# A decoder kernel with another order of norms and distance pieces in its time-warping stage, and a quantised feed-forward written as one pipeline over 16 token tiles

## The chip, the core and the metric

The kernel runs on one core of a Trainium2 chip. The metric is the device time of one launch in microseconds, the median over several runs. Five engines matter: PE (TensorE, matrix products and transposes, results in PSUM), DVE (VectorE), ACT (ScalarE), POOL (GpSimd) and SP (SyncE, which here only issues DMAs). They run independently and wait for each other through semaphores.

## The reference, cut to what matters

Two layers are computed on x (4 batches, 512 tokens, 256 features) with a context of 4 x 1024 tokens. The change touches the first and the last of four sublayers.

```python
# layer 0, cross part: dynamic time warping of layernorm(x) (512) against the context (1024)
D = sqrt(maximum(aa + bb - 2.0 * (a @ b.T), 0))      # aa, bb: squared norms of the rows
row[j] = D[i, j] + minimum(minimum(up, left), diag)  # 512 rows, a scan along 1024 columns
# backtrack the cheapest path, add the rows of one along it to the other, gated

# layer 1, feed-forward: everything is rounded to 4-bit floats in blocks of 16
scale = maximum(max(abs(xb)) / 6, 1e-12)             # per block of 16 features
q(x)  = sign(x) * grid(abs(x / scale)) * scale
h = silu(q(layernorm(x)) @ q(w_gate).T) * (q(layernorm(x)) @ q(w_up).T)   # 704 wide
x = x + tanh(g) * (q(h) @ q(w_down).T)
```

Between them lie a causal self-attention with a mixture of experts and a masked cross-attention, which the change leaves alone.

## The kernel before

The program is a row of blocks (`nc.Block()`). In a block each engine has its own hand-written list of instructions; the next block starts when all engines have finished theirs.

**The time-warping front.** After the inputs have been transposed, `dtw_block` runs `layer_norm` (DVE) on x, turns the result with `transpose_tokens` into `xnT` (scaled by -2), and then runs `dtw_norms`, a block of its own: DVE squares pieces of 512 columns, PE sums them over partitions with a stationary operand of two columns, DVE adds a constant row. The norms of the context go out to memory and come back as one number per partition and lane (`norms`); those of x stay as `rows_j`.

**The distances and the scan** share one block, `dtw_costs`. The 512 rows of x are "slots". They are worked on in cuts of `WIDE` = 112 slots (112, 112, 112, 112, 64). A cut has RB = 33 distance tiles. A tile is 8 PE products of 32 stationary columns each, placed side by side in the array (four batches x two halves of the features), and 4 more that add `rows_j`; four PSUM buffers hold tiles. For the first cut DVE adds the norm and clips (L357), ACT takes the root (L460). For later cuts ACT does both (`rectify` L449, `root` L456). Then ACT's queue stores the cut to memory (`store`, L439), and SP loads it back in chunks of CH = 16 slots in another layout (L316), since the scan runs skewed over 32 lanes per batch.

The scan is DVE's: a turn works off one chunk, 36 turns in all, each 16 times a minimum, a lane shuffle and a scan, with the path rules of the chunk before mixed in. After each turn ACT copies the chunk's decisions away (`keep`, L430 and L432). DVE may not write the decisions of the next turn but one before that is done (`kept`). ACT's list is written out: 11 rectifies ahead of each keep in three turns, the four roots and the store in the fourth.

**The feed-forward.** `fp4_ffn` loads the weights, normalises x, and rounds eight pieces in one block with `quantize` (`ffq_`): four of weights and four of x (1024 wide each). `Quantizer` is spread over three engines for each piece: DVE finds the maxima, scales and inverts them (`scale`, L1873 to L1876); POOL multiplies x by the inverse and the sign by the maximum (`divide`, L1901 and L1905); ACT gives sign and absolute value; DVE rounds by three instructions (`grade`, L1882 to L1884); POOL multiplies the two halves (`combine`, L1911). `lead` says how many pieces `scale` runs ahead of `grade`, and the buffers are lead + 1. Then `turn_rows` transposes the weights and `transpose_tokens` the rounded x.

After that a loop of four passes (`nc.Fori(0, B)`) takes a batch each, as four token tiles of 128: PE makes gate and up products in two halves of 352 columns (L2064), ACT silu (L2106), DVE multiplies (L2130), the quantiser with lead 1 and two buffers rounds the 704 hidden features (`ffb_`), PE transposes them (L2077), ACT copies (L2117 to L2122), PE multiplies with the down weights (L2087), DVE adds to x (L2140).

Of the kernel before, what the change touches and what calls it, by code (L numbers as in the profile page):

```python
# [158 lines left out]
def dtw_block(nc, d, x_sb, ident, ctxT, ctxT_d):  # L159
# [3 lines left out]
    norms_d = nc.dram_tensor("ctx_norms", [1, B * PADI], F32).ap()  # L163
    with ExitStack() as es:
        near = es.enter_context(nc.sbuf_tensor("near", [P, RB, TROW], F16))
        above = es.enter_context(nc.sbuf_tensor("above", [P, RB, TROW], F16))
        with ExitStack() as es1:
            xnT = es1.enter_context(nc.sbuf_tensor("xnT", [P, DH, B * S], F32))
            with ExitStack() as es2:
# [4 lines left out]
            rows_j = es1.enter_context(nc.sbuf_tensor("rows_j", [2, B, S], F32))  # L174
            norms = es1.enter_context(nc.sbuf_tensor("norms", [P, RB], F32))
            dtw_norms(nc, d, xnT, ctxT, rows_j, norms, norms_d)
            dtw_costs(nc, d, dist, near, above, xnT, ctxT, ctxT_d, rows_j, norms, x_sb)
# [3 lines left out]
def dtw_norms(nc, d, xnT, ctxT, rows_j, norms, norms_d):  # L181

    with ExitStack() as es:
        sq = es.enter_context(nc.sbuf_tensor("sq", [P, 2, 2, 512], F32))
        ones2 = es.enter_context(nc.sbuf_tensor("ones2", [P, 2, 2], F32))
        add2 = es.enter_context(nc.sbuf_tensor("add2", [2, 2], F32))
        rows_i = es.enter_context(nc.sbuf_tensor("rows_i", [2, B, PADI], F32))
        ps_n = [es.enter_context(nc.psum_tensor(f"ps_n{i}", [P, 512], F32)) for i in range(2)]
        consts = es.enter_context(nc.semaphore("d_consts"))
        squared = es.enter_context(nc.semaphore("squared"))  # L190
        normed = es.enter_context(nc.semaphore("normed"))
        norm_kept = es.enter_context(nc.semaphore("norm_kept"))
        filled = es.enter_context(nc.semaphore("d_filled"))
        stored = es.enter_context(nc.semaphore("d_norms_stored"))
        spread = es.enter_context(nc.semaphore("d_norms_spread"))

        jobs = [(0, b, c, 1.0) for b in range(B) for c in range(0, SK, 512)] + [(1, b, 0, 0.25) for b in range(B)]
        with nc.Block() as block:
            def keep_norm(dve, n):
                w, b, c, f = jobs[n]  # L200
                if n == 0:
                    dve.wait_ge(consts, 32)
                    dve.wait_ge(filled, 2)
                dve.wait_ge(normed, n + 1)
                dst = rows_j[:, b, :] if w else rows_i[:, b, LEAD + c:LEAD + c + 512]
                nc.vector.tensor_scalar(dst, ps_n[n % 2][0:2, :], add2[:, w:w + 1], None,
                                        ALU.add).then_inc(norm_kept, 1)

            @block.sync
            def _(sp):  # L210
                sp.dma_start(ones2[:], d["c_ones2"]).then_inc(consts, 16)
                sp.dma_start(add2[:], d["c_add2"]).then_inc(consts, 16)
                sp.wait_ge(norm_kept, 2 * B)
                sp.wait_ge(filled, 2)
                sp.dma_start(norms_d, rows_i[0:1, :, :].rearrange("o b i -> o (b i)")).then_inc(stored, 16)
                sp.wait_ge(stored, 16)
                sp.dma_start(norms[:, :], norms_d.rearrange("o (p r) -> (o p) r", r=RB)).then_inc(spread, 16)
                sp.wait_ge(spread, 16)

            @block.gpsimd  # L220
            def _(pool):

                nc.gpsimd.memset(rows_i[:, :, :], 1.0).then_inc(filled, 1)
                pool.wait_ge(filled, 1)
                nc.gpsimd.memset(rows_i[0:1, :, 0:LEAD], FAR2).then_inc(filled, 1)

            @block.vector
            def _(dve):
                for n, (w, b, c, f) in enumerate(jobs):
                    if n >= 2:  # L230
                        dve.wait_ge(normed, n - 1)
                    for h in range(DH):
                        src = xnT[:, h, b * S:(b + 1) * S] if w else ctxT[:, b, h, LEAD + c:LEAD + c + 512]
                        i = nc.vector.scalar_tensor_tensor(sq[:, n % 2, h, :], src, f, src, ALU.mult, ALU.mult)
                    i.then_inc(squared, 1)
                    if n >= 1:
                        keep_norm(dve, n - 1)
                keep_norm(dve, len(jobs) - 1)

            @block.tensor  # L240
            def _(pe):
                pe.wait_ge(consts, 32)
                for n, (w, b, c, f) in enumerate(jobs):
                    pe.wait_ge(squared, n + 1)
                    if n >= 2:
                        pe.wait_ge(norm_kept, n - 1)
# [2042 lines left out]
```

## Time and profile before

| | |
|---|---|
| median of 3 runs | 2692.8 us (2691.69 to 2695.81) |
| the profiled execution | 2694.47 us |
| its span (first to last instruction) | 2692.7 us |
| mean granted TensorE clock | 0.784 of full speed |
| busy share of the span | PE 66%, DVE 61%, ACT 36%, POOL 10% |

The profiled execution took 1.8 us more than its span. The shares are averages over stages that are bound by different engines, so what a change in one stage is worth has to be read from that stage's own stretch of the trace. PE's clock has two levels, 1.2 GHz (0.5 in the profile) and 2.4 GHz (1.0).

### The profile page before, as it was taken

The page shows a single profiled execution, that of the slowest core. Times are in us where ns is not written, and L with a number is a line of the kernel's source. Part 1 is how long each engine was busy: PE and PEld are TensorE (multiplying, and loading weights), DVE is VectorE, ACT ScalarE, POOL GpSimd, SP SyncE. Part 2 cuts the span into 40 slices and gives each one's busy share as a digit, 9 for nine tenths or more (in the row PEclk, how much of TensorE's full clock was granted, in tenths as well). Part 3 has the DMA queues.
Part 4 walks back from the last instruction along what each step waited for, and adds up shares of the span by engine and source line. Part 5 has one row for each costly group of instructions (what it writes and reads, how often), then busy time and mean ns, then how long its engine had stood idle before and what let it go on. Part 6 is the DMA issues. An engine that isn't in the chain of part 4 may idle for free. (4 is left out here: it accounts for less than half of the span.)

```text
span 2692.7 us, 39964 instructions
## 1 busy us (share of the span) xinstructions
PE 1789.7 (66%) x13193; PEld 1032.5 (38%) x13272; DVE 1647.0 (61%) x6787; ACT 982.2 (36%) x1794; POOL 260.3 (10%) x224
## 2 busy tenths in 40 slices
PE   5989500170837888832979507999999999604675
PEld 2445300010724555421656405444544543303453
DVE  5397899898658888440101146767667676286544
ACT  1244522220015666500212002666666666313322
POOL 0000000000000000013000220000000000064432
PEclk8555555555958999955989857999999999857888
DMA  3211100300010000025041122100100000100000
GB/s 96 110 61 51 70 28 28 109 0 1 16 45 9 9 9 2 1 81 192 24 146 49 49 78 86 55 2 1 56 1 25 1 1 1 33 0 0 0 0 31
DMA packets 60244, 104.90 MB, mean 39 GB/s; under 512 B 7449, under 2 KB 42703, under 8 KB 58407
## 3 DMA queue, kind: packets, MB, share of 16 engines
q1 hardware_dynamic: 42654, 72.91, 7.9%
q10 hardware_dynamic: 14352, 22.28, 2.3%
q0 software_dynamic: 3072, 7.53, 0.9%
q8 instruction: 100, 1.64, 0.3%
q14 instruction: 66, 0.54, 0.1%
HBM read 70.72 MB, written 32.85 MB: 38 GB/s over the span
## 5 line engine op out<-in xcount | busy, mean ns | idle before, releaser
L1026 DVE CUSTOM_DVE_ANT_0 xam_junk<-xam_s,xa_mask_q 128x512 bf16<-128x512 f32 x512 | 339.7, 687 | 170.2 <-PE xam_s L933 169.6
L1099 ACT ACTIVATE xam_exp<-xam_s 128x512 f32<-128x512 f32 x512 | 299.6, 598 | 204.1 <-PE xam_s L967 167.6
L933 PE MATMUL xam_s<-xa_kT,xa_qT 96*128 96x512 bf16 x512 | 198.4, 391 | 16.6 <-DVE xam_max L1026 11.1
L964 PE MATMUL xam_s<-xa_qT,xa_kT 99*128 99x512 bf16 x512 | 196.9, 385 | 14.2 <-ACT xam_exp L1099 13.3
L635 PE MATMUL ps_e<-near,start_terms 128*128 128x512 f16 x66 | 27.7, 420 | 211.8 <-DMA lag<-c_lag 204.5
L967 PE MATMUL xam_s<-xa_mask_k,identb 128*128 128x512 bf16 x433 | 165.2, 381 | 0.0
L389 DVE TENSOR_TENSOR_SCAN cost<-m,cost,dist_chunk 128x33 f32<-128x33 f32 x576 | 164.1, 285 | 0.0
L333 PE MATMUL ps_d<-xnT,ctxT 128*32 128x112 f32 (+1 forms) x2640 | 151.5, 379 | 18.0 <-ACT stage L449 7.9
L1026 DVE CUSTOM_DVE_ANT_0 l0m_junk<-l0m_s,l_tri_q 128x128 bf16<-128x128 f32 (+3 forms) x256 | 118.7, 488 | 42.8 <-PE l0m_s L933 40.1
L978 PE MATMUL xam_o<-xam_exp,xa_vt 128*32 128x512 f32 x1024 | 137.2, 605 | 0.0
L1548 PE MATMUL ex_up<-ex_xT,ex_w 128*128 128x512 f32 x256 | 117.0, 616 | 17.6 <-DVE ex_xT L1580 12.0
L1099 ACT ACTIVATE l0m_exp<-l0m_s 128x512 f32<-128x512 f32 (+3 forms) x256 | 104.1, 439 | 60.9 <-PE l0m_s L967 59.3
L378 DVE TENSOR_TENSOR m<-cost 128x33 f32<-128x33 f32 x576 | 109.4, 190 | 20.8 <-DMA dist_chunk<-dist 14.0
L850 POOL COPY l_stk<-l_stk 128x256 bf16<-128x256 bf16 x32 | 21.0, 657 | 1012.1 <-DVE l_stk L829 1012.1
L1580 DVE TENSOR_SCALAR ex_xT<-ex_t,moe_vecs 128x512 f32<-128x512 f32 x16 | 12.2, 805 | 171.7 <-PE ex_t L1535 96.6
L333 PEld LDWEIGHTS ps_d<-xnT,ctxT 128*32 128x32 f32 x2640 | 90.6, 161 | 68.2 <-issue 45.9
L1559 PE MATMUL ex_dn<-ex_w,ex_hm 128*128 128x256 f32 x512 | 111.5, 379 | 0.0
L964 PEld LDWEIGHTS xam_s<-xa_qT,xa_kT 99*128 99x128 bf16 x512 | 50.7, 99 | 140.4 <-ACT xam_exp L1099 99.5
L933 PE MATMUL l0m_s<-l_kT,l_qT 96*128 96x128 bf16 (+3 forms) x256 | 79.8, 317 | 36.0 <-DVE l0m_max L1026 25.9
L1559 PEld LDWEIGHTS ex_dn<-ex_w,ex_hm 128*128 128x128 f32 x512 | 97.2, 191 | 13.6 <-issue 1.0
L430 ACT COPY near<-chunk_near 128x528 f16<-128x528 f16 x37 | 39.9, 1078 | 158.9 <-DVE chunk_near L351 157.3
L635 PEld LDWEIGHTS ps_e<-near,start_terms 128*128 128x128 f16 x66 | 6.8, 102 | 228.5 <-DMA lag<-c_lag 204.7
(324 smaller groups left out, 3900.4 us busy)
## 6 DMA issues: line engine op xcount, KB each, us to landing
dist_chunk<-dist SPq DMA_DIRECT2D x36, 264.0 KB
ex_w<-L_ffn_W ACTq DMA_DIRECT2D x8, 1024.0 KB, 15.1
ex_w<-L_ffn_W SPq DMA_DIRECT2D x8, 1024.0 KB, 16.3
xa_mask<-mask_BxSxS_ik SPq DMA_DIRECT2D x4, 2048.0 KB, 11.1
ctx_nat<-ctx ACTq DMA_DIRECT2D x4, 1024.0 KB, 14.5
x_sb<-x SPq DMA_DIRECT2D x2, 2048.0 KB, 12.3
ctxT_d<-ctxT SPq DMA_DIRECT2D x4, 1024.0 KB, 9.5
ctx_rows<-ctx SPq DMA_DIRECT2D x1, 4096.0 KB, 15.5
```

What stands on the lines that cost most here:

```text
L333: nc.tensor.matmul(o[b], ctxT[:, b, h, k:PADI:RB], xnT[:, h, b * S + a:b * S + z], start=(h == 0), stop=False, tile_position=(0, 32 * b))
L378: nc.vector.tensor_tensor(m[:, u, :], w[:, src, 0:RB], w[:, src, 1:PITCH], ALU.min).then_inc(minned[h], 1)
L389: nc.vector.tensor_tensor_scan(w[:, dst, 1:PITCH], m[:, u, :], step[h][:, s, :], w[:, dst, 0:1], ALU.min, ALU.add).then_inc(scanned[h], 1)
L430: nc.scalar.copy(near[:, :, bass.ds(at, CH)], kept_n[buf][:, :, :].rearrange("p s r -> p r s"))
L933: nc.tensor.matmul(ps1[n % 2][:, 0:w], qT[0:STK, slot(g, h), qt * P:(qt + 1) * P], kT[0:STK, slot(g, h), f * 512:f * 512 + w], start=True, ...
L964: nc.tensor.matmul(o[:, q0:512], kT[:, slot(g, h), kt * P:(kt + 1) * P], qT[:, slot(g, h), q0:512], start=True, stop=False)
L967: nc.tensor.matmul(o[:, q0:q0 + w], identb[:, :], heads.bias_k(g, kt), start=False, stop=True).then_inc(scored2, 1)
L978: nc.tensor.matmul(pso[32 * h:32 * h + 32, q0:512], vt[:, kt, slot(g, h), :], ebuf[n % NE][:, q0:512], start=(kt == 0), stop=(kt == kt_n - 1),
L1026: nc.vector.tensor_tensor_reduce(junk[:, n % NJ, 0:w], ps1[n % 2][:, 0:w], heads.bias_q(g, qt, f), 1.0, NEG * 4, ALU.add, ALU.max, mx[:, g ...
L1099: nc.scalar.activation(ebuf[at % NE][:, q0:512], ps2[at % 2][:, q0:512], ACT.Exp).then_inc(exped, 1)
L1548: last = nc.tensor.matmul(pu[k % 4][:, :], w1[i][:, h, c * P:(c + 1) * P], xT[i % 2][:, h, :], start=(h == 0), stop=(h == DH - 1))
L1559: last = nc.tensor.matmul(pd[k % 2][:, 0:D], hm[i % 2][:, c, t * P:(t + 1) * P], w2[i][:, c, :], start=(c == 0), stop=(c == FC - 1))
```

## The change

It has two parts.

1. **Time-warping.** `norm_inputs` replaces `layer_norm` and `dtw_norms` for this stage: in one block DVE normalises x while POOL squares the context (8 products of 128 x 1024), PE sums them and ACT copies the sums; SP sends them out and back. The norms of x move into `dtw_costs`: DVE squares `xnT` (4 instructions of 128 x 1024), PE sums them (8 products of 512 columns) between the first four distance tiles and their closing products. The closing part of a tile is one product with 128 stationary columns (`share`) in place of four with 32. The cuts become `WIDTHS` = 48, 64, 80, 96, 112, 112; the first is stored in two pieces, 16 slots and 32. ACT's rectifies, roots and stores are dealt out evenly over the turns (`work`), starting one turn before the scan. The two fills of `w` and `m` go from DVE to POOL.
2. **Feed-forward.** `quantize` keeps the four weight pieces. x stays as normalised rows (`ff_xn`), and the loop of four passes becomes one block over 16 tiles, `ffn_tiles`: each tile has a quantiser job of 256 wide for its x (four tiles ahead) and one of 704 for its hidden features, with lead 2 and five buffers; x is transposed tile by tile.

```diff
-    layer_norm(nc, es2, x_sb, xn, "ln0")
+    norm_inputs(nc, es3, d, x_sb, xn, ctxT, which, rows_i, norms, norms_d, spread)
...
+        @block.gpsimd
+        def _(pool):
+            nc.gpsimd.memset(rows_i[:, 0:LEAD], FAR2).then_inc(filled, 1)
+            for n, (b, h) in enumerate(jobs):
+                if n >= 4:
+                    pool.wait_ge(weighed, n - 3)
+                src = ctxT[:, b, h, LEAD:PADI]
+                nc.gpsimd.tensor_tensor(sq[:, n % 4, :], src, src, ALU.mult).then_inc(squared, 1)
...
+            act.wait_ge(weighed, len(jobs))
+            for c in range(2):
+                nc.scalar.copy(rows_i[:, LEAD + c * 512:LEAD + (c + 1) * 512], ps[c][0:B, :]).then_inc(kept, 1)
...
-                    for b in range(B):
-                        last = nc.tensor.matmul(o[b], one_j[:, :], rows_j[:, b, a:z], start=False, stop=True,
-                                                tile_position=(0, 32 * b))
-                    last.then_inc(prod, 1)
+                def close(n):
+                    a, z = cuts[n // RB]
+                    nc.tensor.matmul(ps[n % 4][:, 0:z - a], share[:, :], rows_j[:, a:z], start=False,
+                                     stop=True).then_inc(prod, 1)
...
+        for q in range(1, len(cuts)):
+            first, turns = cuts[q - 1][0] // CH - 1, WIDTHS[q - 1] // CH
+            items = [("rectify", q * RB + k) for k in range(RB)] + [("root", (q, i)) for i in range(4)] + [("store", q)]
+            for i, item in enumerate(items):
+                work[first + i * turns // len(items)].append(item)
...
-                srcs += [xn[:, 4 * g:4 * g + 4, :].rearrange("p t d -> p (t d)") for g in range(NT // 4)]
...
-            q = Quantizer(nc, nm, [(hid[:, t, :], hq[:, t, :]) for t in range(QT)], FI, 1)
+    order = [("x", t) for t in range(LEAD4)]
+    for t in range(NT):
+        order += [("h", t)] + ([("x", t + LEAD4)] if t + LEAD4 < NT else [])
+    q = Quantizer(nc, nm, [(xn[:, t, :], xn[:, t, :]) if kind == "x" else (hid[:, t % NH4, :], hq[:, t % NH4, :])
+                           for kind, t in order], FI, 2, 5)
...
+            turn_x(0)
+            for t in range(NT + 2):
+                if t + 1 < NT:
+                    turn_x(t + 1)
+                if t < NT:
+                    prods(t)
+                if t >= 2:
+                    turn_h(t - 2)
+                    product(t - 2)
...
+            for t in range(NT):
+                if t >= 3:
+                    add(t - 3)
+                mix(t)
+                for n in begun(t):
+                    grades(n)
+            for n in range(len(order) - q.lead, len(order)):
+                q.grade(dve, n)
```

ACT's list of `ffn_tiles` holds, for tile t, the copy of x tile t + 1, the two silus, the copies of hidden tile t - 2 (`keep_h`), then sign and absolute value of the jobs begun; from t = 12 on `keep_h` stands behind these.

**How the order of instructions moves.** First PE at the start of `dtw_costs`. Before (`ps_d` are the tiles' PSUM buffers):

```order
L333 MATMUL ps_d<-xnT,ctxT 32x112 x8
L336 MATMUL ps_d<-rows_j,one_j 32x112 x4
L333 MATMUL ps_d<-xnT,ctxT 32x112 x8
L336 MATMUL ps_d<-rows_j,one_j 32x112 x4
L333 MATMUL ps_d<-xnT,ctxT 32x112 x8
```

And in the changed kernel (`ps_j` takes the norms of x):

```order
L353 MATMUL ps_d<-xnT,ctxT 32x48 x32
L367 MATMUL ps_j<-x_sb,which_batch 4x512 x8
L359 MATMUL ps_d<-rows_j,share 128x48 x4
L353 MATMUL ps_d<-xnT,ctxT 32x48 x8
L359 MATMUL ps_d<-rows_j,share 128x48
```

Four tiles stand open while the norms of x are summed; the tiles of the first cut are 48 wide instead of 112.

Second, ACT in the same block, from the first store on. Before (`near` and `above` are the keep of a turn):

```order
L439 DMA dist<-x_sb 128x3696
L449 ACTIVATE stage<-ps_d,norms 128x112 x11
L430 COPY near<-chunk_near 128x33x16
L432 ACTIVATE above<-chunk_above 128x33x16
L449 ACTIVATE stage<-ps_d,norms 128x112 x11
L430 COPY near<-chunk_near 128x33x16
L432 ACTIVATE above<-chunk_above 128x33x16
```

And now:

```order
L484 DMA dist<-x_sb 128x528
L484 DMA dist<-x_sb 128x1056
L497 ACTIVATE stage<-ps_d,norms 128x64 x26
L473 COPY near<-chunk_near 128x33x16
L475 ACTIVATE above<-chunk_above 128x33x16
L497 ACTIVATE stage<-ps_d,norms 128x64 x7
L504 ACTIVATE stage<-stage 128x528 x4
L484 DMA dist<-stage 128x2112
L473 COPY near<-chunk_near 128x33x16
L475 ACTIVATE above<-chunk_above 128x33x16
L497 ACTIVATE x_sb<-ps_d,norms 128x80 x10
```

26 rectifies of the second cut now stand ahead of the first keep, and from the third cut on 10 or fewer ahead of each.

Third, POOL in the feed-forward, in the middle of a pass before (`ffb_hid`, `ffb_hq`: hidden features and their rounded form):

```order
L1901 TENSOR_TENSOR ffb_v<-ffb_hid,ffb_inv 128x704
L1905 TENSOR_TENSOR ffb_sgn<-ffb_sgn,ffb_amax 128x704
L1911 TENSOR_TENSOR ffb_hq<-ffb_hi,ffb_sgn 128x704
L1901 TENSOR_TENSOR ffb_v<-ffb_hid,ffb_inv 128x704
L1905 TENSOR_TENSOR ffb_sgn<-ffb_sgn,ffb_amax 128x704
```

And in a tile of the changed kernel (`ff_xn`: x, rounded in place):

```order
L1953 TENSOR_TENSOR ffb_v<-ffb_hid,ffb_inv 128x704
L1957 TENSOR_TENSOR ffb_sgn<-ffb_sgn,ffb_amax 128x704
L1963 TENSOR_TENSOR ffb_hq<-ffb_hi,ffb_sgn 128x704
L1953 TENSOR_TENSOR ffb_v<-ff_xn,ffb_inv 128x256
L1957 TENSOR_TENSOR ffb_sgn<-ffb_sgn,ffb_amax 128x256
L1963 TENSOR_TENSOR ff_xn<-ffb_hi,ffb_sgn 128x256
```

Each tile's three long products are followed by three short ones of the x four tiles ahead.

## Rows read from the trace of the kernel before

**Rows 1.** Busy time by stretch (start:end, length, each engine's busy us and instructions, PE's clock).

```profile
26.50:39.30 12.80, 0.02 (x1) 0.05 (x1) 12.07 (x50) 1.50 (x2) 0.00 (x0) 0.55 0.00 1
39.30:46.60 7.30, 6.38 (x32) 6.15 (x32) 2.77 (x4) 2.39 (x4) 0.02 (x1) 0.62 0.01 2
46.60:74.40 27.80, 24.01 (x48) 3.35 (x48) 22.99 (x36) 0.00 (x0) 3.79 (x2) 0.94 0.01 1
74.40:124.00 49.60, 48.42 (x808) 26.26 (x808) 15.96 (x35) 13.33 (x33) 0.00 (x0) 0.51 0.28 109
...
2364.50:2452.00 87.50, 0.00 (x0) 0.00 (x0) 69.49 (x48) 16.66 (x16) 60.94 (x24) 0.50 0.00 0
...
2465.00:2519.90 54.90, 38.09 (x136) 25.78 (x136) 27.62 (x36) 16.57 (x31) 19.33 (x12) 0.87 0.00 0
```

**Rows 2.** Timeline of DVE, ACT's queue and SP, first distance tile to first scan step.

```profile
77.16 0.42 DVE L357 TENSOR_SCALAR x_sb<-ps_d,norms 128x112 f32<-128x112 f32 x1 [0.39 <-PE ps_d L336]
...
124.13 0.35 ACTq L439 DMA_DIRECT2D dist<-x_sb  x1
...
132.08 74.64 SPq L316 DMA_DIRECT2D dist_chunk<-dist  x9
...
137.63 0.20 DVE L378 TENSOR_TENSOR m<-cost 128x33 f32<-128x33 f32 x1 [13.96 <-DMA dist_chunk<-dist]
```

**Rows 3.** Timeline of SP: the context norms go out and come back.

```profile
66.30 0.23 SPq L215 DMA_DIRECT2D ctx_norms<-rows_i  x1
67.99 0.35 SPq L217 DMA_DIRECT2D norms<-ctx_norms  x1
```

**Rows 4.** Timeline of ACT: a rectify of the 64-wide cut (in brackets its wait).

```profile
300.94 0.38 ACT L449 ACTIVATE x_sb<-ps_d,norms 128x64 f32<-128x64 f32 x1 [0.58 <-PE ps_d L336]
```

**Rows 5.** Busy time by stretch: PE products with 128 stationary, 8 moving columns (L1374).

```profile
1171.00:1184.60 13.60, 13.47 (x64) 13.47 (x64) 0.00 (x0) 0.00 (x0) 0.00 (x0) 0.51 0.71 292
```

**Rows 6.** Timeline of POOL: one product of 128 x 1024.

```profile
2408.94 1.93 POOL L1901 TENSOR_TENSOR ffq_v<-ffw_xn,ffq_inv 128x1024 f32<-128x1024 f32 x1 [2.15 <-DVE ffq_inv L1876]
```

**Rows 7.** DVE's longest waits in the scan (total us, times, longest), and its end.

```profile
DVE best L348 <- ACT above L432: 24.2, 5, 5.9
...
509.19 0.20 DVE L351 TENSOR_TENSOR chunk_near<-best,cost 128x66 f16<-128x66 f32 x1
```

**Rows 8.** Timeline of DVE and POOL in the rounding of the weights.

```profile
2366.23 0.20 DVE L1874 TENSOR_SCALAR ffq_amax<-ffq_amax 128x80 f32<-128x80 f32 x1
...
2368.50 1.13 DVE L1874 TENSOR_SCALAR ffq_amax<-ffq_amax 128x80 f32<-128x80 f32 x1
...
2367.21 2.36 POOL L1901 TENSOR_TENSOR ffq_v<-ffw_rows,ffq_inv 128x1280 f32<-128x1280 f32 x1 [129.76 <-DVE ffq_inv L1876]
```

**Rows 9.** DVE groups of the feed-forward loop (out<-in, count, busy us, mean ns).

```profile
L1883 DVE TENSOR_TENSOR ffb_v<-ffb_v,ffb_hi 128x704 f32<-128x704 f32 x16 | 32.4, 2023 | 0.5
L1884 DVE TENSOR_TENSOR ffb_hi<-ffb_v,ffb_hi 128x704 f32<-128x704 f32 x16 | 22.8, 1424 | 0.6
```

**Rows 10.** Timeline of DVE and POOL in the loop's first pass.

```profile
2477.13 1.39 POOL L1901 TENSOR_TENSOR ffb_v<-ffb_hid,ffb_inv 128x704 f32<-128x704 f32 x1 [25.25 <-DVE ffb_inv L1876]
...
2488.54 0.89 DVE L1873 TENSOR_REDUCE ffb_amax<-ffb_hid 128x44 f32<-128x704 f32 x1 [2.11 <-POOL ffb_hq L1911]
...
2496.32 0.89 DVE L1873 TENSOR_REDUCE ffb_amax<-ffb_hid 128x44 f32<-128x704 f32 x1 [0.99 <-POOL ffb_hq L1911]
...
2504.99 0.89 DVE L1884 TENSOR_TENSOR ffb_hi<-ffb_v,ffb_hi 128x704 f32<-128x704 f32 x1
```

**Rows 11.** Timeline of POOL (last weight piece) and PE (loop) in the feed-forward.

```profile
2416.62 3.15 POOL L1911 TENSOR_TENSOR ffw_down<-ffq_hi,ffq_sgn 128x1408 f32<-128x1408 f32 x1 [3.22 <-DVE ffq_hi L1884]
2460.52 3.69 PE L118 MATMUL ffT_ps<-ident,ffw_xn 128*128 128x128 f32 x32 [0.60 <-PEq L1953]
2474.23 1.35 PE L2064 MATMUL ffb_g<-ff_wguT,ffb_xb 128*128 128x352 f32 x4
2507.59 2.95 PE L2087 MATMUL ffb_y<-ff_wdT,ffb_hqT 128*128 128x256 f32 x12
```

More of the change, by code:

```diff
@@ L173, in dtw_block @@
                 transpose_tokens(nc, es2, xn, lambda g, h: xnT[:, h, g * 512:(g + 1) * 512], ident, "xT", mul=-2.0)
[L174 to L177, printed above, removed]
+            dtw_costs(nc, d, dist, near, above, xnT, ctxT, ctxT_d, which, norms, spread, x_sb)
@@ L178, in dtw_block @@
         backtrack(nc, d, near, above, spans, x_sb, ident)
[L181 to L246, printed above, removed]
-                    for h in range(DH):
-                        last = nc.tensor.matmul(ps_n[n % 2][0:2, :], ones2[:, w, :], sq[:, n % 2, h, :],
-                                                start=(h == 0), stop=(h == DH - 1))
-                    last.then_inc(normed, 1)
@@ L262, in dtw_costs @@
+def dtw_costs(nc, d, dist, near, above, xnT, ctxT, ctxT_d, which, norms, spread, x_sb):
     with ExitStack() as es:
@@ L293, in dtw_costs @@
         LAST = 2 * CH
-        cuts = [(a, min(a + WIDE, S)) for a in range(0, S, WIDE)]
+        cuts = [(sum(WIDTHS[:q]), sum(WIDTHS[:q + 1])) for q in range(len(WIDTHS))]
+        work = {n: [] for n in range(-1, NCH)}
+        for q in range(1, len(cuts)):
[3 more added lines that the diff above has]
+                work[first + i * turns // len(items)].append(item)
         with nc.Block() as block:
@@ L317, in _, with tiles @@
                 sp.wait_ge(spilled, 16 * B)
+            @block.gpsimd
+            def _(pool):
+                nc.gpsimd.memset(m[:, :, :], FAR).then_inc(blank, 1)
+                nc.gpsimd.memset(w[:, :, :], FAR).then_inc(blank, 1)
             @block.tensor
             def _(pe):
-                pe.wait_ge(told, 16)
-                for n in range(len(cuts) * RB):
-                    q, k = n // RB, n % RB
-                    a, z = cuts[q]
+                def tiles(n):
+                    (a, z), k = cuts[n // RB], n % RB
                     if n >= 4 + RB:
@@ L426, in _ @@
                 nc.scalar.nop().then_inc(kept, 2)
+                act.wait_ge(normed, 1)
+                nc.scalar.copy(rows_j[:, :], ps_j[0:B, :]).then_inc(jnormed, 1)
                 def keep(buf, at):
@@ L1830, with __init__ @@
 class Quantizer:
-    def __init__(self, nc, nm, jobs, width, lead):
+    def __init__(self, nc, nm, jobs, width, lead, bufs=None):
         self.nc, self.jobs = nc, jobs
-        self.lead, self.bufs = lead, lead + 1
+        self.lead, self.bufs = lead, bufs or lead + 1
         self.amax = nm.sb("amax", [P, self.bufs, width // QB])
```

399 lines of the change are left out of this document (264 added, 135 removed).

## The prediction, made before the changed kernel was run

> **What bounds the kernel now.** I read the page first, then the busy time of the two stretches that the diff touches, then their timelines engine by engine.
>
> In the front, [rows 1] show one engine at a time. DVE normalises for 12.8 us while PE and POOL stand still, the transposes take 7.3 us, and the block of the norms 27.8 us, in which DVE and PE hand each other single pieces. Then come the tiles of the first cut: PE is busy for 48.42 of 49.60 us, at half clock. An fp32 product is two instructions, so 808 of them are 33.7 tiles of 24, and a tile takes 1.44 us. Nothing of the scan can start meanwhile. The first clip is at 77.2 us, the first cut's store at 124.1, its load at 132.1 and the first scan step at 137.6 [rows 2]: store 8.0 us, load 5.5.
>
> From there DVE is the bound. The last turn ends at 509.2, and DVE's only large waits are five for ACT's `keep`, 24.2 us [rows 7], since 11 rectifies paced by PE stand ahead of it. So a turn alone takes (509.4 - 137.6 - 24.2) / 36 = 9.65 us.
>
> At the end, rounding the eight pieces takes 87.5 us and a pass of four tiles 54.9, of which PE works 38.1, DVE 27.6, ACT 16.6 and POOL 19.3 [rows 1]: no engine is full; the chain is, with fill and drain in every pass. Inside a pass two maxima follow each other after 7.78 us [rows 10]: the steady step of a hidden tile.
>
> **A bound shared by DVE and POOL.** In [rows 8] the same tiny DVE instruction takes 0.20 us alone and 1.13 us where a POOL product is under way, and it ends 0.06 us after that product. The three-instruction rounding shows the same: its second and third average 2.02 and 1.42 us [rows 9] and take 0.89 undisturbed [rows 10]. The maxima (0.89 both times) are not held up. I therefore count products of POOL and DVE's two-input or plain SBUF instructions as excluding each other.
>
> **Change 1, up to the first cut.** POOL's 8 products of 128 x 1024 at 1.93 us [rows 6] take 15.4 us from 26.7, so to about 42; PE needs 16 products of 512 columns, 1.0 us each (24.01 us for 24, [rows 1]) or nearly twice that at half clock. Two pairs at half clock and six at full one bring it to 47. Two ACT copies (1.3) and the two small DMAs (1.7 between their issues, [rows 3], plus 0.4 of issue) end the block at 50.4, against 39.3. DVE's 12.8 us lie under it, with room for 8 us of exclusion. Transposes: 58, where `dtw_costs` started at 74.4.
> There, eight products of 512 columns now stand between tiles and closing products; half at each clock they cost 8 x 1.25 = 10, after 2.1 us of tiles, plus 1.3 for copy and signals: first clip at about 72, not 77. DVE's squares (4 x 1.2) run ahead of PE, and POOL's fills lie beside them.
> A tile's price: 112 wide 1.44 us, 64 wide 0.96 [rows 4], so 0.32 + 0.01 per column for twelve products. Eight products of 48 are 0.53. The closing product with 128 stationary columns is not in the trace at such a width. Nearest: [rows 5], 8 moving columns at half clock, 13.47 / 64 = 0.21 per instruction, 0.42 for the pair. Lower bound 0.27 (what the four small ones cost at 48), upper 0.16 + 0.42 = 0.58, if stream and load add up. I take 0.42, from the row with the same stationary operand. Tile: 0.96 at 48, 1.06 at 64, 1.17 at 80, 1.28 at 96.
> The Trainium skill, "TensorE: Matmul & The Clock Gate", Part 3 (The mechanism), says that a weight load passes a running product only where row groups differ. Were loads never hidden, the closing product would cost the upper bound, and the sum would be 21 us worse (rival C).
> So the store goes out at 72 + 1.7 + 29 x 0.96 + 0.9 = 102.4, not 124.1. Its first piece is 264 KB in place of 1848; I take 3 us to land (from 1.7 for a tiny one to 8.0), and 5.5 for the load: scan starts at 111, **27 us sooner**.
>
> **The scan.** With T0 = 102 the scan starts at T0 + 9 and has data for three turns, to T0 + 38. The second cut needs 33 x 1.06 = 35 us of PE, 2.5 of roots, then about 5.5 to store and 5.5 to load: T0 + 48.5. That is a **new stall of 10.5 us**. ACT's 26 rectifies ahead of the first keep end at T0 + 27 and the keep at 29, just when turn 2 wants it. Third cut: 38.6 us more of PE, 3.0 roots, 11.2 transfers, T0 + 88, needed at T0 + 87: 1 us. Later cuts need 42 or 46 us of PE in turns of 48 to 68 us, with 6 to 8 rectifies (at most 4 of them waited for) before a keep: none. So 12 us of waits in place of 24: **12 us saved**, 39 in all.
>
> **Change 2.** Rounding the weights: the last product of the down weights ends at 2419.8, 55.3 after the start, with two x pieces' multiplications and scales in between (4 POOL products of 1.93 or more, about 11 with what hangs on them). So 44 us remain of 87.5: **43.5 saved**. The transposes of x (2460.5 to 2465.0, [rows 11]) go: **4.5 saved**. The loop was 4 x 54.8 less the last restart, 216 us from 2465.0 to the last addition.
> The new loop, DVE in iteration t: its own work for a hidden tile is 27.6 / 4 = 6.9, less what the rounding was held up, (32.4 + 22.8) / 16 - 2 x 0.89 = 1.7: 5.2 us. The x job scales three of its parts by 256/704: about 1.9. Sum 7.1. POOL: 3 x 1.39 + 3 x 0.6 = 6.0. Exclusive parts: 6.0 + DVE's 3.3 = 9.3, the lower bound of a step. The upper is 7.1 + 6.0 = 13.1, no overlap. In order: addition and two multiplications 1.4 (POOL only finishes its x product), maximum and inverse 1.5 (POOL idle: it has nothing to divide yet), rounding of the tile before with POOL's two products between, 4.9, then x: maximum 0.45, a wait for POOL's long product 1.0, inverse and three roundings with two short products between, 2.5. Together **11.8 us**; the h-only step of 7.78 had the same pattern. PE has 4 x 1.2 for the products, 0.9 and 0.3 of transposes, 2.9 down [rows 11]: 8.9 at full clock, hidden, as are ACT's 5.
> Fill: two x jobs through the quantiser 8.5 us (PE's second transposes wait for job 1), the first tile 8, then 12.6 to the second, since PE's next transpose stands behind x job 2, which POOL combines after the first hidden tile. Then 11 steps of 11.8 = 130. In the last steps `keep_h` stands behind sign and absolute value, so PE's next products wait for the product before: 11, 11, and 17.4 for the last, whose PE list holds `turn_h(12)`, rounded only with tile 14. Drain after the last multiplication: three roundings, two down products in series, 21.5. Sum 8.5 + 8 + 12.6 + 130 + 39.4 + 21.5 = 220: **4 us longer than the four passes**. Change 2 saves 43.5 + 4.5 - 4 = **44 us**.
>
> **Sum.** 39 + 44 = 83 us off 2692.7. The profiled execution (2694.5) lies 1.7 us above the median of 2692.8, so I take the difference off the median: **2610 us**.
>
> **Rivals.**
> A. *The locks overlap better* than my list: step 9.3 to 10.5, 11 x 2 = 20 us less: 2588. For it: POOL can use DVE's maxima, inverses and additions, 3.5 us a step. Against: it has no work then, except the x product.
> B. *PE's clock rises in the tiles.* At 2.4 GHz a tile of 48 costs half, the first cut 14 us less, and the 10.5 us stall goes: 2585. Against: 0.5 throughout 49.6 us of full work [rows 1].
> C. *Closing product at 0.58.* First cut 29 x 0.16 = 5 later, second cut 5 more, third 5, fourth and fifth 3 each: 21, 2631. The page's rule above gives the same.
> D. *More stalls between blocks or in the lists* (norms at half clock throughout, 10 us; keep late by a turn): 2625.
> E. *Slower than before: PE's clock stays at half in the tile loop.* Its 8.9 us become 17.8, with 0.9 of copies 18.7 > 11.8, and PE sets the step: 15 x 18.7 + 36 = 317, 97 us more: 2707. It decides from a step of 17.5 on. Against: with 38.1 busy of 54.9 a pass still had 0.87 [rows 1]; PE's gap of 3 us a step could cost some half-clock stretches, which the slack takes.
> F. The change does nothing: not credible, 43.5 us of work leave a chain.
>
> **Chances.** My sum 0.42 (2598 to 2620), A 0.15, B 0.06, C 0.15, D 0.15, E 0.03, others on either side 0.04. The range 2575 to 2638 leaves out E and half of the extremes. A measurement of this kernel tells 0.2%, 5.4 us, from no change; so faster 0.96, same 0.015, slower 0.025.
>
> **What would show it.** First clip at 70 to 74 us, scan start at 108 to 114, a wait of DVE for `dist_chunk` before turn 3 near 10 us and the wait for `keep` below 3; closing tiles 0.96 us apart at 48 wide. In the loop the additions 11.8 us apart, rounding instructions at 2 us beside POOL products, PE's clock at 1.0. The rounding block near 44 us. Wrong would be: a step at PE's 8.9 or above 13, a tile at 1.12, a first clip after 77.

## The result, and the profile after

| | before | changed |
|---|---|---|
| median | 2693.6 us (4 runs) | 2628.5 us (4 runs, 2625.4 to 2633.3) |
| the profiled execution | 2694.5 us | 2625.4 us |
| its span | 2692.7 us | 2623.7 us |
| busy share of the span | PE 66%, DVE 61%, ACT 36%, POOL 10% | PE 71%, DVE 63%, ACT 37%, POOL 11% |

The ratio of the medians is 0.976 (95% interval 0.974 to 0.978): 65 us less, where 83 were forecast. The range held it; the forecast's own time, 2610, was 18 us too low. By the landmarks of the two traces (DVE's first product of the backtracking, 518.2 and 480.6 us; the experts' first transpose, 1252.6 and 1215.9; their last product, 1518.3 and 1491.5; the last addition, 2681.3 and 2612.3) the difference is 37.6 us behind the scan, 36.7 ahead of the experts, 26.8 behind them and 69.0 at the end. So the front gave 37.6 (forecast 39), the feed-forward 42.6 (44, from 2366.5 and 2340.1 us, the weights' first inverse, to the end), and the experts, whose code is untouched, took 10 back.

Busy time by stretch, for [rows 1]: the norms, the transposes, distance tiles up to the first store, the rounding of the weights, the tile loop (start:end, length, PE, PEld, DVE, ACT, POOL, PE's clock).

```profile
26.50:45.50 19.00, 14.83 (x32) 2.13 (x32) 17.44 (x47) 1.27 (x3) 13.76 (x8) 1.00 0.01 2
45.50:51.80 6.30, 5.29 (x32) 5.08 (x32) 2.77 (x4) 2.34 (x4) 0.00 (x0) 0.73 0.02 3
51.80:93.80 42.00, 40.84 (x627) 28.85 (x628) 14.36 (x37) 9.87 (x35) 1.97 (x2) 0.63 0.32 128
2338.20:2382.00 43.80, 0.00 (x0) 0.00 (x0) 35.84 (x24) 8.65 (x8) 32.21 (x12) 0.50 0.00 0
2390.00:2612.80 222.80, 161.08 (x576) 105.39 (x576) 171.18 (x240) 69.89 (x161) 116.71 (x96) 0.87 0.00 1
```

The norms run at full clock, which the forecast had only for a part: the block takes 19 us, not 24. The rounding takes 43.8 us (forecast 44), the loop 222.8 (220).

DVE's timeline from the first clip on (start, length, in brackets the wait and who ended it), for [rows 2] and [rows 7]:

```profile
61.73 0.90 DVE L398 TENSOR_SCALAR x_sb<-ps_d,norms 128x48 f32<-128x48 f32 x4 [4.94 <-PE ps_d L359]
...
74.88 0.30 DVE L398 TENSOR_SCALAR x_sb<-ps_d,norms 128x48 f32<-128x48 f32 x1 [0.77 <-PE ps_d L359]
75.96 0.30 DVE L398 TENSOR_SCALAR x_sb<-ps_d,norms 128x48 f32<-128x48 f32 x1 [0.77 <-PE ps_d L359]
...
101.44 0.20 DVE L419 TENSOR_TENSOR m<-cost 128x33 f32<-128x33 f32 x1 [8.01 <-DMA dist_chunk<-dist]
...
126.81 0.26 DVE L386 TENSOR_TENSOR best<-cost 128x99 f32<-128x99 f32 x1 [4.75 <-ACT above L475]
...
144.93 0.20 DVE L419 TENSOR_TENSOR m<-cost 128x33 f32<-128x33 f32 x1 [9.57 <-DMA dist_chunk<-dist]
...
190.75 0.20 DVE L419 TENSOR_TENSOR m<-cost 128x33 f32<-128x33 f32 x1 [7.12 <-DMA dist_chunk<-dist]
...
240.46 0.20 DVE L419 TENSOR_TENSOR m<-cost 128x33 f32<-128x33 f32 x1 [1.56 <-DMA dist_chunk<-dist]
```

The first clip is at 61.7 (forecast 72), a tile 48 wide follows the other after 1.07 to 1.08 us (forecast 0.96), and in the later cuts after 1.21, 1.34 and 1.47 us at 64, 80 and 96 wide (forecast 1.06, 1.17 and 1.28). The scan starts at 101.4 (forecast 111, before 137.6). Then come waits of 4.75, 9.57, 7.12 and 1.56 us, 23.0 together, where 12 were forecast and 24.2 stood before. Three of the four are for data: the scan eats a cut faster than PE makes the next one.

One step of the tile loop, DVE and POOL, for [rows 8] to [rows 10]:

```profile
2478.94 1.62 POOL L1953 TENSOR_TENSOR ffb_v<-ffb_hid,ffb_inv 128x704 f32<-128x704 f32 x1 [2.13 <-DVE ffb_inv L1928]
2479.36 1.95 DVE L1935 TENSOR_TENSOR ffb_v<-ffb_v,ffb_hi 128x704 f32<-128x704 f32 x1
2480.53 2.03 POOL L1957 TENSOR_TENSOR ffb_sgn<-ffb_sgn,ffb_amax 128x704 f32<-128x704 f32 x1
2481.34 1.96 DVE L1936 TENSOR_TENSOR ffb_hi<-ffb_v,ffb_hi 128x704 f32<-128x704 f32 x1
2483.44 1.67 POOL L1963 TENSOR_TENSOR ffb_hq<-ffb_hi,ffb_sgn 128x704 f32<-128x704 f32 x1 [0.89 <-issue]
2483.67 1.47 DVE L1926 TENSOR_SCALAR ffb_amax<-ffb_amax 128x16 f32<-128x16 f32 x1
2487.09 0.47 DVE L2250 SCALAR_TENSOR_TENSOR x_sb<-ffb_y,ff_gate,x_sb 128x256 f32<-128x256 f32 x1
...
2498.26 0.47 DVE L2250 SCALAR_TENSOR_TENSOR x_sb<-ffb_y,ff_gate,x_sb 128x256 f32<-128x256 f32 x1
```

DVE's and POOL's ends alternate (2480.56, 2481.31, 2482.56, 2483.30, 2485.11, 2485.14), and DVE's scaling of 16 maxima per partition lasts 1.47 us. The additions are 11.17 us apart (forecast 11.8).

### The profile page after: what moved, and what is told of

Same layout as the page of the kernel before. It is cut to its first block and busy times, and to the rows that moved or that the text cites. A ratio compares the mean times of both kernels' runs of the same rounds, so it can differ in the third digit from the quotient of the medians.

```text
span 2623.7 us, 39283 instructions
## 1 busy us (share of the span) xinstructions
PE 1852.2 (71%) x12876; PEld 1103.4 (42%) x12876; DVE 1653.3 (63%) x6821; ACT 983.9 (37%) x1859; POOL 283.9 (11%) x269
## 5 line engine op out<-in xcount | busy, mean ns | idle before, releaser
L1019 PE MATMUL xam_s<-xa_mask_k,identb 128*128 128x512 bf16 x512 | 195.3, 381 | 0.0
L353 PE MATMUL ps_d<-xnT,ctxT 128*32 128x112 f32 (+4 forms) x3168 | 158.2, 348 | 9.8 <-ACT stage L497 8.6
L359 PE MATMUL ps_d<-rows_j,share 4*128 4x112 f32 (+4 forms) x396 | 140.8, 457 | 0.8 <-ACT rows_j L469 0.8
L1600 PE MATMUL ex_up<-ex_xT,ex_w 128*128 128x512 f32 x256 | 122.1, 637 | 22.6 <-DVE ex_xT L1632 13.1
L359 PEld LDWEIGHTS ps_d<-rows_j,share 4*128 4x128 f32 x396 | 97.1, 303 | 49.1 <-issue 45.7
L353 PEld LDWEIGHTS ps_d<-xnT,ctxT 128*32 128x32 f32 x3168 | 97.1, 160 | 40.2 <-issue 17.4
```

Source lines behind the costliest of these rows:

```text
L353: nc.tensor.matmul(ps[n % 4][32 * b:32 * b + 32, 0:z - a], ctxT[:, b, h, k:PADI:RB], xnT[:, h, b * S + a:b * S + z], start=(h == 0), stop= ...
L359: nc.tensor.matmul(ps[n % 4][:, 0:z - a], share[:, :], rows_j[:, a:z], start=False, stop=True).then_inc(prod, 1)
L1019: nc.tensor.matmul(o[:, q0:q0 + w], identb[:, :], heads.bias_k(g, kt), start=False, stop=True).then_inc(scored2, 1)
L1600: last = nc.tensor.matmul(pu[k % 4][:, :], w1[i][:, h, c * P:(c + 1) * P], xT[i % 2][:, h, :], start=(h == 0), stop=(h == DH - 1))
```

## The experiments

Each kernel was timed beside the kernel before on the same chip, whose medians over the calls were 2693.6 to 2695.1 us. Gains below are differences of medians.

### e1, e2: each part alone

e1 keeps the changed `dtw_block` and takes `fp4_ffn` of before; e2 the other way round.

> The changed time-warping front with the feed-forward of before. Theory (the two parts are independent and the 10 us that the changed kernel lost in the expert stage, 211 to 221 us from its first transpose on, are not caused by either): the front alone saves 37.6 us as in the changed kernel's trace, 2656 us; the expert stage takes 265 to 276 us from its first transpose to its last product, wherever. Rival 1 (the front's change causes the loss in the expert stage): 2666 us in every run, and the expert stage at 276. Rival 2 (my forecast, 39 us from the front): 2654, not to be told from the first by time, but by the stalls in the scan: forecast 10.5, 1 and 0 us, seen in the changed kernel 9.6, 7.1 and 1.6.

> The time-warping front of before with the changed feed-forward. Theory: the feed-forward alone saves 42.7 us as in the changed kernel's trace (forecast: 44), 2651 us, with the expert stage as before (266 us from its first transpose to its last product). Rival: the expert stage loses 10 us here too, so the loss does not come from the front: 2661.

e1: 2670.6 us, ratio 0.991 (0.988 to 0.995), 23.5 us less. e2: 2651.7 us, ratio 0.984 (0.981 to 0.987), 42.3 us less. They add to 65.8, the whole gain. The stalls in e1's scan are 9.9, 7.0 and 1.8 us, and its backtracking starts 36.2 us sooner than before; its expert stage takes 275.8 us, that of e2 266.6. So the loss among the experts comes with the front's change: rival 1 of e1.

### e3: the closing part as four small products

```diff
-                    nc.tensor.matmul(ps[n % 4][:, 0:z - a], share[:, :], rows_j[:, a:z], start=False,
-                                     stop=True).then_inc(prod, 1)
+                    for b in range(B):
+                        last = nc.tensor.matmul(ps[n % 4][32 * b:32 * b + 32, 0:z - a], share[:, 32 * b:32 * b + 32],
+                                                rows_j[:, a:z], start=False, stop=True, tile_position=(0, 32 * b))
+                    last.then_inc(prod, 1)
```

> The changed kernel, but the closing part of a distance tile is four products with 32 stationary columns again (the same four rows of norms, each product takes its own 32 columns of share). Theory (the closing product with 128 stationary columns is what makes tiles dear: 1.07 us at 48 wide instead of 0.80, 1.21 instead of 0.96 at 64, 1.34 instead of 1.12 at 80): first clip near 62, scan start at 92.5 instead of 101.4, second cut lands at 128 instead of 144.9, its stall 6.4 instead of 9.6, the stalls of 7.1 and 1.6 gone, end of the scan at 446 instead of 474: 27 us less, 2601. Rival (the four rows of norms or the order of tile and closing part make it dear, not the width of the stationary operand): tiles stay at 1.07 and 1.21, no change, 2628.

2605.0 us, ratio 0.968 (0.965 to 0.971), 23.5 us less than the changed kernel. PE's timeline of e3, cut 48 wide at half clock, and its only gap without a releaser:

```profile
66.49 0.39 PE L353 MATMUL ps_d<-xnT,ctxT 128*32 128x48 f32 x6
70.09 0.48 PE L353 MATMUL ps_d<-xnT,ctxT 128*32 128x48 f32 x10 [3.21 <-issue]
...
84.90 0.39 PE L360 MATMUL ps_d<-rows_j,share 4*32 4x48 f32 x8
85.21 0.56 PE L353 MATMUL ps_d<-xnT,ctxT 128*32 128x48 f32 x16
85.70 0.39 PE L360 MATMUL ps_d<-rows_j,share 4*32 4x48 f32 x8
```

A tile takes 0.80 us as extrapolated in the forecast from [rows 4], at 64 wide 0.96. With 0.53 us for the other eight products, an estimate of the forecast, the closing part costs 0.27 us in this form and 0.54 in the changed kernel's. At 64, 80 and 96 wide the tiles are 0.96, 1.12 and 1.28 us apart, against 1.21, 1.34 and 1.47. The stalls are 6.0 and 0.5 us, the wait for `keep` is gone. The backtracking starts at 461.4 us, 19 sooner and not 27: this execution's first clip came 1.8 us later and the gap of 3.2 us stood in the first cut.

### e4: the old widths in the changed kernel

```diff
-WIDTHS = (48, 64, 80, 96, 112, 112)
-STORES = (0, 16, 48, 112, 192, 288, 400)
+WIDTHS = (112, 112, 112, 112, 64)
+STORES = (0, 112, 224, 336, 448)
```

> The changed kernel with the cuts of before: 112, 112, 112, 112, 64 slots, each stored whole; everything else as changed. Theory (with a closing product this dear narrow cuts give at the scan's start what they take back in stalls): a tile of 112 takes 1.61 us, first store at 109, scan start at 122 to 124 instead of 101.4, but no stall for the second cut and no long wait for keep, so the scan ends at 122.8 + 36 x 9.65 = 470 to 475, where it ended at 473.8: 2625 to 2631, the same. Rival (the narrow first cuts are what the front's gain comes from): 21 us later start, 21 us longer, 2649.

2616.8 us, ratio 0.972 (0.969 to 0.975): 12 us less than the changed kernel. The scan starts at 114.6 us, later by 13, and has no further wait of the kinds above; the backtracking starts at 470.3, 10 sooner than with narrow cuts. A tile takes 1.61 us at half clock, as the theory had it, but 0.95 at full clock, which PE kept until 73 us in this execution. It was the fastest of the four, 8 us below their median, so these 10 us need not hold for the others. The expert stage takes 265.9 us, not 275.6. The theory's 2625 to 2631 is missed by some ten us, the rival's 2649 by 32. With the dear closing product the narrow cuts bring nothing; in e9 below, with seven stores as in the changed kernel, the wide ones are still 7.5 us ahead, but the two intervals (0.971 to 0.976 and 0.974 to 0.978) overlap, and PE's clock, which differs between executions, has a part in that.

### e5, e6: POOL's product of sign and maximum

e5 does only 32 of its 704 columns, so the scaling of the other signs is left out. e6 does all of it, behind the x job:

```diff
+                late = n + 1 < len(order) and order[n][0] == "h" and order[n + 1][0] == "x"
+                if not late:
+                    signs(n)
                 if n >= q.lead:
                     combine(n - q.lead)
+                if order[n][0] == "x" and n and order[n - 1][0] == "h":
+                    signs(n - 1)
```

> The changed kernel, but the product of sign and maximum of a hidden tile on POOL works on 32 of its 704 columns only, so the sign's scaling of the rest is left out; all waits stay. Theory (products of POOL and DVE's SBUF instructions exclude each other, and the two together set the step of 11.17 us): the 1.4 us of that product go out of the step, which falls to 9.8; DVE's last rounding instruction of a hidden tile (1.96 us behind that product) falls to 0.9; twelve such steps and the last ones make 16 to 20 us, 2610. Rival (the step is set by the chain division, absolute value, rounding, and 1.96 us is what the rounding instruction takes; the product lies beside it): the step stays at 11.2, 2628.

> The changed kernel with the same products, but POOL's product of sign and maximum of a hidden tile comes behind the three products of the x job that follows, so it falls into the 2.13 us in which POOL waits while DVE adds, multiplies out of PSUM and takes the maxima. Theory (exclusion): it fits beside those DVE instructions, the step falls from 11.17 by 1.0 to 1.4 us to about 9.9, and the rounding instruction from 1.96 to 0.9 us: 12 to 17 us less, 2613. Rival (no exclusion, or DVE's reads of PSUM are held up as well): the step stays or the additions and multiplications grow by the same 1.4: 2628.

e5 2611.3 us, ratio 0.969 (0.966 to 0.972), 17 us less than the changed kernel; e6 2614.8 us, ratio 0.971 (0.968 to 0.974), 14 less. In both the additions are 10.10 us apart. POOL and DVE in a step of e6:

```profile
2480.80 1.39 POOL L2279 TENSOR_TENSOR ffb_sgn<-ffb_sgn,ffb_amax 128x704 f32<-128x704 f32 x1
2482.99 1.62 POOL L2285 TENSOR_TENSOR ffb_v<-ffb_hid,ffb_inv 128x704 f32<-128x704 f32 x1 [0.79 <-DVE ffb_inv L1928]
```

```profile
2485.39 0.89 DVE L1936 TENSOR_TENSOR ffb_hi<-ffb_v,ffb_hi 128x704 f32<-128x704 f32 x1
```

The rounding instruction takes 0.89 us as soon as no POOL product of that length is ahead of it, and POOL's product takes 1.39, not 2.03, beside DVE's addition, multiplications and maximum. The step loses 1.07 us, the extra length of that one DVE instruction, whether the product is cut or only moved. It holds the other way round too. In e5 POOL's product of 32 columns lasts 0.89 us, where one of 256 takes 0.62 in the same step, and ends at 2487.74, 0.10 behind a DVE instruction that ends at 2487.64:

```profile
2485.68 1.96 DVE L1935 TENSOR_TENSOR ffb_v<-ffb_v,ffb_hi 128x704 f32<-128x704 f32 x1
2486.85 0.89 POOL L1959 TENSOR_TENSOR ffb_sgn<-ffb_sgn,ffb_amax 128x32 f32<-128x32 f32 x1
```

The exclusion is shown; my 1.4 was the product's length, while the wait that it caused is 1.07.

### e7: both ends of the tile loop

From tile 13 on a hidden tile is rounded one tile after its maxima, so that `keep_h` always stands ahead of sign and absolute value on ACT; PE makes tile 0's products first. The core of it, of PE's and of ACT's list (`alternate` begins a tile's jobs and ends those that a table lists for it, on all three engines):

```diff
+            prods(0)
             for t in range(NT + 2):
                 if t + 1 < NT:
                     turn_x(t + 1)
-                if t < NT:
+                if 0 < t < NT:
                     prods(t)
...
-                if t in range(2, NT - LEAD4):
+                if t >= 2:
                     keep_h(t - 2)
-                for n in begun(t):
-                    grades(n)
-                if t == NT - 1:
-                    for n in range(len(order) - q.lead, len(order)):
-                        q.absolute(act, n)
-                if t >= NT - LEAD4:
-
-                    keep_h(t - 2)
+                alternate(t, grades, lambda n: q.absolute(act, n))
```

> The changed kernel with other lists at the two ends of the tile loop: from tile 13 on a hidden tile is rounded one tile after its maxima instead of two jobs later, so keep_h always stands ahead of the sign and absolute value; and PE makes the products of tile 0 ahead of the transposes of x tile 1. Theory (the last steps of 13.6, 12.0 and 19.8 us and the drain are waits of the lists for each other): the three fall to 8 to 9 us each and the fill by 3, 20 to 25 us less, 2605. Rival (at the ends PE's clock or its products are the bound): under 8 us less, 2621.

2607.9 us, ratio 0.968 (0.965 to 0.972), 20.6 us less. The additions of the last five tiles, 10.9, 21.0, 20.2, 4.2 and 4.2 us apart in the changed kernel, are 11.6, 12.5, 12.8, 5.7 and 4.2 apart, 13.8 us less together; the one before them fell from 8.8 to 7.3, and the first addition comes 3.0 us sooner, counted from the weights' first inverse. The waits were those of the lists.

### e8, e9: where the experts' 10 us come from

e8 is the kernel before once more. e9 is e4 with the first cut stored in three pieces:

```diff
-STORES = (0, 112, 224, 336, 448)
+STORES = (0, 16, 48, 112, 224, 336, 448)
```

> The kernel before once more, for a second profile. The expert stage (first transpose of the experts to their last product) took 266 us in the profile of before and 275 to 276 in those of the changed kernel and of its front alone. Theory 1 (it is one of two lengths that come by chance from run to run): 266 or 275 here. Theory 2 (the narrow cuts bring it): 266 again.

> The changed kernel with the cuts of before (112, 112, 112, 112, 64 slots), as in e4, but the first cut is stored in three pieces (16, 32 and 64 slots), so ACT's queue carries seven stores as in the changed kernel, and 288 packets more than in e4. It is for the expert stage, 264 to 267 us in the four profiles with five stores and 274 to 276 in the six with seven. Theory (what ACT's queue carried before shifts how its later issues wait: in the expert stage the third weight issue of ACT came 12.8 us after the first transpose with five stores and 7.3 to 7.9 with seven, and the last ended 3 us later): 274 to 276 here, with that pattern; the scan starts some 4 us earlier than in e4, since its first chunk comes from a small store: 2616.8 - 4 + 9 = 2622. Rival (the cuts' widths or the instruction count do it): 264 to 267, 2613.

e8: 2693.9 us, expert stage 263.9. e9: 2621.0 us, ratio 0.974 (0.971 to 0.976), expert stage 275.2. So neither chance nor the widths. With five stores on ACT's queue (before, e2, e4, e8, and e11 and e12 below) the stage takes 263.9 to 266.6 us, with seven (the changed kernel, e1, e3, e5, e6, e7, e9, e10) 273.8 to 276.0, fourteen profiles without an exception. What differs shows on ACT's queue. Its issues of expert weights and biases in the kernel before:

```profile
1254.67 0.46 ACTq L1512 DMA_DIRECT2D ex_w<-L_ffn_W  x1
1255.29 9.97 ACTq L1515 DMA_DIRECT2D ex_b<-L_ffn_b  x1
1265.42 0.39 ACTq L1512 DMA_DIRECT2D ex_w<-L_ffn_W  x1
1265.97 4.27 ACTq L1515 DMA_DIRECT2D ex_b<-L_ffn_b  x1
1270.33 1.28 ACT L1524 ACT_TABLE_LOAD   x1 [84.48 <-issue]
```

And in the changed kernel:

```profile
1217.60 0.46 ACTq L1564 DMA_DIRECT2D ex_w<-L_ffn_W  x1
1218.22 5.42 ACTq L1567 DMA_DIRECT2D ex_b<-L_ffn_b  x1
1223.81 6.61 ACTq L1564 DMA_DIRECT2D ex_w<-L_ffn_W  x1
1230.58 5.77 ACTq L1567 DMA_DIRECT2D ex_b<-L_ffn_b  x1
1236.44 1.28 ACT L1576 ACT_TABLE_LOAD   x1 [87.42 <-issue]
```

Counted from the experts' first transpose (1252.57 and 1215.86), ACT is done with issuing after 17.7 us before and 20.5 now; only then does it begin with the activations that PE waits for. PE's first such wait, before and in the changed kernel:

```profile
1272.37 7.97 PE L1548 MATMUL ex_up<-ex_xT,ex_w 128*128 128x512 f32 x14 [3.57 <-ACT ex_hm L1524]
```

```profile
1238.48 2.08 PE L1600 MATMUL ex_up<-ex_xT,ex_w 128*128 128x512 f32 x2 [4.08 <-ACT ex_hm L1576]
```

They start 19.8 and 22.6 us behind the first transpose. The second group of four experts begins 3.7 us later and loses another 3.2 in the same way (its last issue ends 156.3 and 163.2 us behind the first transpose), and PE works at half clock for longer (mean granted clock of the stage 0.94 and 0.92). The queue had carried 5168 packets up to the experts instead of 4880. That two more stores shift which of the later issues wait, and by how long, is shown by e9 against e4. By what mechanism the queue does it, and whether the number of stores or that of packets counts, no run tells.

e9 also shows something else. PE's clock in the first cut of e4 and e9 (PE, PEld, DVE, ACT, POOL, clock):

```profile
75.00:80.00 5.00, 5.00 (x66) 3.41 (x62) 1.45 (x4) 1.22 (x3) 0.00 (x0) 0.50 0.02 3
```

```profile
75.00:80.00 5.00, 5.00 (x96) 3.74 (x92) 2.14 (x5) 2.28 (x6) 0.00 (x0) 1.00 0.01 3
```

The same tiles ran at 1.2 GHz from 73 us on in e4 and at 2.4 GHz to 100 us and beyond in e9. The last clip of the first cut came at 90.7 us there and at 102.1 in e4, 11.4 sooner by the clock; the scan started at 101.6, 13 us sooner, since its first chunk also came from a smaller store. Its five executions lie between 2602 and 2628 us, the profiled one being the fastest.

### e10 to e12: the parts together

e10 joins e3, e6 and e7 with cuts of 64, 64, 80, 96, 96, 112 (seven stores). e11 has five cuts and five stores instead:

```diff
+WIDTHS = (80, 96, 112, 112, 112)
+STORES = (0, 80, 176, 288, 400)
```

e12 issues the copies of the context later:

```diff
-                for b in range(B):
-                    sp.dma_start(ctxT_d[b], ctxT[:, b, :, LEAD:PADI]).then_inc(spilled, 16)
...
                     sp.dma_start(step[h][:, :, :].rearrange("p s r -> p (s r)"), src).then_inc(loaded[h], 16)
+                    if 2 <= n < 2 + B:
+                        sp.dma_start(ctxT_d[n - 2], ctxT[:, n - 2, :, LEAD:PADI]).then_inc(spilled, 16)
```

> Closing part as four small products (e3), late sign (e6), both ends of the tile loop (e7), and cuts of 64, 64, 80, 96, 96, 112 with seven stores. Theory (the gains add): 2605 (e3) less 20.6 (e7), less 12 (e6, fewer steps of the tail are left to it), less 3 (no stall for the second cut): 2569; the expert stage at 275. Rival (late sign and the shorter tail gain the same time): 2580.

> As e10, but five cuts (80, 96, 112, 112, 112) each stored whole, so that ACT's queue carries five stores as before the change. Theory (the count of stores sets the expert stage): the scan starts 5 us later than in e10, no stalls, and the expert stage falls from 275 to 266: 2564. Rival (it does not): 2574.

> As e11, but the four transfers that copy the transposed context to memory (1 MB each, at the start of the distance block) are issued between the chunk loads of turns 2 to 5. Theory (they filled the DMA engines from 55 to 70 us and held PE's next instructions back, as in the gap of 3.2 us in e3): no gap of PE before 75 us, up to 3 us less where e11 has such a gap, the same where not; chunk loads 3 to 5 come at most 3 us later, hidden. Rival (the transfers now delay the stores and loads of the second cut, and DVE waits for them): 3 to 8 us more.

e10 2573.7 us, ratio 0.955 (0.954 to 0.957), between theory (2569) and rival (2580): 54.8 us below the changed kernel, where e3, e6 and e7 add to 57.8; e11 2569.2, ratio 0.954 (0.952 to 0.956); e12 2567.7, ratio 0.953 (0.951 to 0.955). In e11 the expert stage is back at 264.3 us, 11.5 us shorter than in e10, while the scan starts 5.8 later (111.1 for 105.3): together 5.7 us, of which the medians show 4.5. The theory's 5 us below e10 came (its 2564 was counted from e10's forecast of 2569), the rival's 5 above did not. The gap of PE without a releaser, 2.8 us in e10 and 2.0 in e11 while the copies filled the DMA engines, is not there in e12; the scan starts 44.9 us behind the first clip there, in e11 47.6. The medians show 1.5 us of that; their intervals overlap, and the four runs of each (2569.1 to 2570.7 and 2566.4 to 2568.9) only just don't. e12 is 127 us below the kernel before in the same call and 61 below the changed one.

## Why the prediction held, and where it was off

The sum was 27 + 12 + 43.5 + 4.5 - 4 = 83 us. Its terms, measured:

**Up to the scan, 27: was 36.** Two steps were off against each other. The norms and the squares of x ran at full clock throughout; "two pairs at half clock" and "half at each clock" took too low a clock. The block of the norms ended at 45.5 us for 50.4, the transposes at 51.8 for 58, and the first clip came 9.9 us behind them for 14: 10 us sooner than forecast. The tiles then cost more: of the closing product "I take 0.42, from the row with the same stationary operand", and it is 0.54 (1.07 less 0.53 for the eight products). The upper bound of 0.58, stream and load added, was nearly it; e3 with four small products shows that the width of the stationary operand does it. By the rule of the Trainium skill, "TensorE: Matmul & The Clock Gate", Part 3 (The mechanism), that a weight load passes a running product only where row groups differ, it would cost that upper bound; the measured 0.54 lies nearer to it than to 0.42.

**The scan's waits, 12: was 1.** The stall before turn 3 was forecast as 10.5 us and is 9.57, but the third cut's was forecast as 1 us and is 7.12, the fourth's as none and is 1.56, and the wait for `keep` is 4.75 instead of under 3. All of it fits the same mis-sized term: 0.11, 0.15, 0.17 and 0.19 us more a tile at 48, 64, 80 and 96 wide, 33 tiles a cut. Together the two parts of the front gave 37.6 for 39, and that they came so near is luck: 9 us more in one part stand against 11 less in the other. A turn is 9.71 us, not 9.65, since the last one's closing products end at 511.4 and not at 509.2; that holds before and after alike. The earlier start was partly handed on: what the scan gained at its head it waited for later, since PE hardly stood still from the first tile to the end of the fourth cut (35.0 of 35 us busy from 75 to 110, 89.7 of 90 from 110 to 200, 29.0 of 29 from there to 229). Rival C named the mechanism, and its 0.16 us more a tile is near the 0.11 to 0.19 measured. Its price of 21 us did not come in full: with the first clip 10.3 us sooner the forecast's own sum would give 49.3 for the front, and 37.6 is 11.7 less.

**The feed-forward, 44: was 42.6.** The rounding block went from 87.5 to 43.8 us, the transposes of x went, the loop is 222.8 us for 216. Inside, the steady step was 11.17 us for 11.8; a longer fill and the last steps (13.6, 12.0 and 19.8 us between POOL's divisions for 11, 11 and 17.4) took that back. The exclusion of DVE and POOL, read from a 0.20 us instruction that took 1.13 [rows 8], was right, as e5 and e6 show. The Trainium skill, "SBUF — State Buffer", section "SBUF: two separate sides", says the same, that the pair of ports that VectorE and GpSimd share is locked for a whole instruction; the 1.96 us that became 0.89 agree.

**The rest of the program, 0: was -10.** No step of the prediction looked at what ACT's queue hands on to later stages. These 9.9 us are the larger part of the 18, and e9 with e4 shows that two more stores bring them. Of the rest 2.8 are in the terms above (37.6 and 42.6 for 39 and 44), 1.3 in small differences elsewhere (37.6 against 36.7, 26.8 against 26.4), and 3.9 lie between the profiled executions (69.0 us apart) and the medians (65.1).

Rival A (a step of 9.3 to 10.5) did not come by itself, but e6 reached it by moving one product. Rival B came in part: the clock stayed high to 63 us in the changed kernel, and in e9 for the whole first cut. E did not: PE's clock was 0.87 in the loop, where the forecast looked for 1.0, and with PE busy for 161 of 222.8 us the step had room for that.

## What to carry to other kernels

A narrower first piece starts a consumer sooner, but it pays only as far as the producer keeps ahead: compare the producer's time per piece with the consumer's at each width before choosing, fixed cost included. A joint that makes one wide product out of four small ones is no saving when a stationary operand four times as wide has to be loaded for it. Where two engines exclude each other, put the work of one beside those instructions of the other that don't need the shared side; and after a change in the number of DMAs on a queue look at the queue's issues in all later stages, not only in the changed one.

## What was not expected of the hardware

- Two more stores on ACT's queue at 100 us (288 packets) cost 7 to 12 us in a stage at 1200 us, in each of eight profiles against each of six.
- While 4 MB went out at some 410 GB/s with all DMA engines busy, PE stood still for 3.2, 2.8 and 2.0 us without waiting for any semaphore (e3, e10, e11); with the copies moved the gap was gone. The changed kernel, e1, e4, e5, e6, e7 and e9 had the copies and no gap. What parts the two is the closing part: the three with a gap make it of four small products, so a tile is 24 matrix instructions and not 18, and PE works through its list faster. All three gaps stand at the same place of PE's list, behind the 134th matrix instruction of the tiles and the 64th of the closing parts, whatever the width and the time. The profile also lists packets of 16 KB on a queue of the kind "instruction": one falls into the half microsecond from 67.5 us in e3 (gap 66.9 to 70.1), from 69.5 in e10 (69.1 to 71.9) and from 67.5 in e11 (68.0 to 70.1). That instructions arrived late fits all of this; it is not shown, since no row tells whose instructions a packet carried.
- With PE hardly idle from the first tile on (one wait of 0.8 us) its clock fell to 1.2 GHz at 63 us in the changed kernel and between 66 and 68 in e1, e5, e6 and e7, which have the same front; with the 112 wide tiles it fell at 73 in e4 and not before 105 in e9. What decides it stays open. It moves the end of the first cut by 11 us between e4 and e9.
